# A four-stage token mixer on one core: weight setup that overlaps its transfers, and another order of the work ahead of the state-space scan

## The reference

```
h = attention(x, w_qkv, b_qkv, w_out, b_out)             # 16 heads of 16
h = concat(cls_tok, h)                                   # 513 tokens
h = h + diag_recurrence(layernorm(h))
h = h + ffn(layernorm(h))          # weights: w -> clip(round(w / mean|w|), -1, 1) * mean|w|
h = h + ssm(layernorm(h))
h = h + gated_ffn(layernorm(h))    # w_gate, w_up, w_down quantised in the same way

def ssm(x):
    x_val, z = split(x @ W_in.T)                         # 512 channels each
    x_val = silu(conv4(x_val) + conv_b)
    dt = softplus(x[:, :, :64] @ W_dt.T + b_dt)
    Bm, Cm = x @ W_B.T, x @ W_C.T                        # 16 states
    # for each token: h = exp(dt * A) * h + (dt * x_val) * B ;  y = h . C
    return (scan(x_val, A, Bm, Cm, dt) * silu(z)) @ W_out.T
```

## Time and profile before

| what | value |
|---|---|
| median of 3 runs | 2579.07 us (2574.51 to 2581.37) |
| the profiled execution | 2572.49 us |
| its span | 2570.7 us, 26879 instructions |
| busy share PE / DVE / ACT / POOL | 83% / 80% / 58% / 45% |
| mean granted TensorE clock | 0.951 of full speed |
| span's start to the first scores (L857) | 61.07 us |
| first `taps` to first scan, turn 0 | 357.39 to 390.70 us |

### The profile page before, as it was taken

The page is one execution under the profiler, slowest core; times in us unless marked ns, Lnnn a source line. Parts: engine busy times, 40 slices in busy tenths (PEclk is TensorE's granted clock), DMA queues, the critical chain, the costliest instruction groups (busy, mean ns, idle before and its releaser), DMA issues.

```text
span 2570.7 us, 26879 instructions
## 1 busy us (share of the span) xinstructions
PE 2139.9 (83%) x9364; PEld 1187.4 (46%) x9364; DVE 2067.8 (80%) x2435; ACT 1479.5 (58%) x2358; POOL 1148.7 (45%) x567
## 2 busy tenths in 40 slices
PE   1998888898799887889779898798977988778896
PEld 0326663345333666434542376543453247544354
DVE  6865979996786588999778557999888747799977
ACT  0563558774365446876527544687553754568744
POOL 1220248992222024998222211699722211279952
PEclk9999998999899999999989999899989999989998
DMA  5300000000220000000022000000003100000000
GB/s 183 93 14 1 1 1 1 1 1 1 71 87 1 1 1 1 1 1 1 1 84 75 1 1 1 0 1 1 1 1 113 46 1 1 1 1 0 1 1 17
DMA packets 41088, 51.46 MB, mean 20 GB/s; under 512 B 9072, under 2 KB 32368, under 8 KB 40944
## 3 DMA queue, kind: packets, MB, share of 16 engines
q1 hardware_dynamic: 40944, 49.62, 6.0%
HBM read 26.25 MB, written 10.49 MB: 14 GB/s over the span
## 4 chain that ended last, share of the span: by engine, by line
DVE 43%; PE 37%; issue 8%; ACT 7%; POOL 3%; DMA 1%; SPq 0%; DVEq 0%; ACTq 0%; POOLq 0%
DVE big L1936 16%; PE psum L737 10%; PE psum L884 5%; ACT big L1177 4%; PE psum L872 3%; PE psum L857 3%; PE psum L800 3%; PE psum L1039 3%; DVE mid L1830 3%; ACT mid L1177 2%; DVE big L1608 2%; PE psum L1071 2%; POOL big L2086 2%; DVE mid L1552 2%; DVE negmax L1660 2%
## 5 line engine op out<-in xcount | busy, mean ns | idle before, releaser
L1177 ACT ACTIVATE big<-psum 128x512 f32<-128x512 f32 (+2 forms) x604 | 455.6, 774 | 264.8 <-PE psum L872 141.7
L2086 POOL TENSOR_TENSOR big<-big 128x2048 f32<-128x2048 f32 x124 | 561.8, 4530 | 38.8 <-DVE big L1936 38.6
L1039 PE MATMUL psum<-big,ident 128*128 128x512 f32 x992 | 506.9, 617 | 65.4 <-POOL big L2086 65.4
L1936 DVE TENSOR_TENSOR_SCAN big<-psum,b,big 128x512 f32<-128x512 f32 x404 | 490.3, 1265 | 6.9 <-ACT psum L1177 6.6
L1660 DVE TENSOR_REDUCE negmax<-psum 128x1 f32<-128x512 f32 x512 | 318.7, 678 | 48.3 <-PE psum L857 47.3
L1177 ACT ACTIVATE psum<-mid,aneg 128x512 f32<-128x512 f32 x404 | 268.5, 681 | 79.9 <-DVE big L1936 79.8
L1039 PEld LDWEIGHTS psum<-big,ident 128*128 128x128 f32 x992 | 174.5, 194 | 231.0 <-POOL big L2086 141.8
L857 PE MATMUL psum<-mid 96*128 96x512 bf16 x512 | 189.9, 391 | 33.6 <-DMA mid<-mid 22.8
L872 PE MATMUL psum<-mid 98*128 98x512 bf16 x512 | 181.9, 382 | 20.1 <-ACT big L1177 14.3
L1177 ACT ACTIVATE mid<-mid 128x513 f32<-128x513 f32 (+3 forms) x120 | 104.3, 883 | 154.7 <-DVE mid L1946 80.6
L2051 POOL TENSOR_TENSOR big<-big,mid 128x513 f32<-128x513 f32 x40 | 50.9, 1284 | 288.8 <-ACT big L1177 288.8
(11 more groups left out here) (222 smaller groups left out, 3931.8 us busy)
## 6 DMA issues: line engine op xcount, KB each, us to landing
mid<-mid SPq DMA_DIRECT2D x192, 64.0 KB, 2.5
mid<-scratch SPq DMA_DIRECT2D x192, 64.0 KB, 2.2
scratch<-big SPq DMA_DIRECT2D x4, 1536.0 KB, 5.6
out<-hres SPq DMA_DIRECT2D x8, 513.0 KB, 4.1
big<-in_x SPq DMA_DIRECT2D x8, 512.0 KB, 5.1
big<-in_w SPq DMA_DIRECT2D x2, 1024.0 KB, 6.1
big<-in_wg SPq DMA_DIRECT2D x1, 1024.0 KB, 9.4
big<-in_wu SPq DMA_DIRECT2D x1, 1024.0 KB, 11.3
```

Of the source, the lines that this page charges most:

```text
L1039: mm = nc.tensor.matmul(y_psum[:, c], ident[:, :], st(1, k)[:, c], start=(n == 0), stop=(n == NS - 1))
L1177: return nc.scalar.activation(o, a, func, **kw)
L1936: V.tensor_tensor_scan(st(0, k)[:, c], decays(DT * k + c), bx, b0[:, p, n, c:c + 1], ALU.mult, ALU.add).then_inc(scanned, 1)
L2086: G.tensor_tensor(st(1, k), st(0, k), c_row(k).unsqueeze(1).broadcast_to([P, DT, S]), ALU.mult).then_inc(hc_ready, 1)
```

## The change

**Setup.** Each raw transfer has its own semaphore, and DVE sums each as it lands. The transfer order is: raw, `wq`, `wk`, `vec`, the input of p = 0, then the other weights and the input of p = 1. `turn_start` for the first turn is signalled as soon as SP has issued the first input. The sum over partitions is a matmul with `mean_w` (all 1/256) into bank 7, ahead of the first products on PE. DVE goes twice over each raw tensor (times inverse, min 1; max -1, plus ROUND), and ACT makes the third pass (minus ROUND into bfloat16) after its copies of the first q and k products. PE's turn and DVE's loop wait for `SETUP_ACT`. ACT's copies of the first q and k products stand in `first_copies`, ahead of the turn (in the loop: at the end of the turn before), so ACT's stream has three turns in a loop and the last one written out.

**Lead-up.** `round_up(0)` stands behind both `split_bc`, and `round_up(1)` behind `step_sizes(0)`. The products x(1), z(0), z(1) are interleaved by `IN_ORDER`, with ACT's readers in an order that fits it. The product of dt and x for p = 0 is made on DVE behind `step_sizes(1)`; the one for p = 1 stays on POOL, but waits for DVE's b0.

```diff
@@ -17,7 +17,6 @@
-RADD = bass.bass_isa.ReduceOp.add
@@ -59,7 +58,8 @@
-SETUP_DVE = 8 + 5 + 2 + 15 + 1
+SETUP_DVE = 8 + 5 + 2 + 10 + 1
+SETUP_ACT = 1 + 5
@@ -89,6 +89,11 @@
+IN_ORDER = [("x0", 1), ("x1", 1), ("z0", 0), ("x2", 1), ("z1", 0), ("x3", 1), ("z2", 0), ("z3", 0)]
+IN_ORDER += [(f"z{c}", 1) for c in range(DT)]
@@ -143,8 +148,7 @@
-    order.extend((f"x{c}", 1) for c in range(DT))
-    each(*[f"z{c}" for c in range(DT)])
+    order.extend(IN_ORDER)
@@ -264,7 +268,7 @@
-        wsum = sb("wsum", [P, 8]); wtot = sb("wtot", [P, 8]); wscale = sb("wscale", [P, 8])
+        wsum = sb("wsum", [P, 8]); wscale = sb("wscale", [P, 8])
@@ -436,7 +440,9 @@
-        raw_in = ctx.enter_context(nc.semaphore("raw_in"))
+        raw_in = [ctx.enter_context(nc.semaphore(f"raw_in{n}")) for n in range(5)]
+        qk_weights_in = ctx.enter_context(nc.semaphore("qk_weights_in"))
+        wtot_full = ctx.enter_context(nc.semaphore("wtot_full"))
@@ -544,10 +550,17 @@
+        raws = [big[:, n * raw_n:(n + 1) * raw_n] for n in range(5)]
+        CLAMPED = [8 + 5 + 2 + n for n in (3, 5, 7, 9, 10)]
...
-        plain = [(wq, "wq"), (wk, "wk"), (wv, "wv"), (wo, "wo"), (wa, "wa"), (wB, "wB"), (wC, "wC"), (wx, "wx"),
+        qk_weights = [(wq, "wq"), (wk, "wk")]
+        n_qk = len(qk_weights) + 1
+        plain = [(wv, "wv"), (wo, "wo"), (wa, "wa"), (wB, "wB"), (wC, "wC"), (wx, "wx"),
...
-        n_plain = len(plain) + 3
+        n_plain = len(plain) + 2
+        wtot = psum[:, 7 * BANK:7 * BANK + 8]
@@ -618,22 +631,24 @@
-            def load_x(turn):
-                for p in range(PAIR):
-                    sp.dma_start(xin[:, p], x[turn * PAIR + p].rearrange("k p q -> p k q")).then_inc(x_in[p], 16)
+            def load_x(turn, p):
+                sp.dma_start(xin[:, p], x[turn * PAIR + p].rearrange("k p q -> p k q")).then_inc(x_in[p], 16)
...
-                             v).then_inc(raw_in, 16)
+                             v).then_inc(raw_in[n], 16)
+            for t, name in qk_weights:
+                sp.dma_start(t[:, :, :], w[name].rearrange("(k p) c -> p k c", p=P)).then_inc(qk_weights_in, 16)
+            sp.dma_start(vec[:, :], w["vec"]).then_inc(qk_weights_in, 16)
+            load_x(0, 0)
+            sp.nop().then_inc(turn_start, 1)
...
-            sp.dma_start(vec[:, :], w["vec"]).then_inc(weights_in, 16)
...
-            load_x(0)
-            sp.wait_ge(setup_dve, SETUP_DVE)
-            sp.nop().then_inc(turn_start, 1)
+            load_x(0, 1)
@@ -695,7 +710,8 @@
-                    load_x(i + 1)
+                    for p in range(PAIR):
+                        load_x(i + 1, p)
@@ -716,10 +732,12 @@
-            pe.wait_ge(setup_dve, SETUP_DVE)
-            pe.wait_ge(weights_in, 16 * n_plain)
+            pe.wait_ge(qk_weights_in, 16 * n_qk)
...
+                pe.wait_ge(setup_dve, SETUP_DVE)
+                pe.wait_ge(setup_act, SETUP_ACT)
+                pe.wait_ge(weights_in, 16 * n_plain)
@@ -977,9 +995,9 @@
-                def inputs(name, wt, p):
-                    for c in range(DT):
-                        fill(f"{name}{c}", p, [(wt[:, k, c * P:(c + 1) * P], big_un(p)[:, k]) for k in range(KT)])
+                def inputs(name, p):
+                    wt, c = (wx if name[0] == "x" else wz), int(name[1])
+                    fill(name, p, [(wt[:, k, c * P:(c + 1) * P], big_un(p)[:, k]) for k in range(KT)])
@@ -987,7 +1005,8 @@
-                inputs("x", wx, 0)
+                for c in range(DT):
+                    inputs(f"x{c}", 0)
@@ -1000,9 +1019,8 @@
-                inputs("x", wx, 1)
-                for p in range(PAIR):
-                    inputs("z", wz, p)
+                for name, p in IN_ORDER:
+                    inputs(name, p)
@@ -1164,6 +1182,8 @@
+            pe.wait_ge(setup_dve, 8 + len(raw_w))
+            nc.tensor.matmul(wtot, mean_w[:, :], wsum[:, :], start=True, stop=True).then_inc(wtot_full, 1)
@@ -1180,14 +1200,23 @@
-            act.wait_ge(weights_in, 16 * n_plain)
-            act.wait_ge(setup_dve, 1)
+            act.wait_ge(qk_weights_in, 16 * n_qk)
+            act.wait_ge(setup_dve, 8)
...
-            act.wait_ge(setup_dve, SETUP_DVE)
-            with act.Fori(0, TURNS) as i:
-                act.wait_ge(turn_start, i + 1)
+            def copy_high(p):
+                for name, c in zip(QK_ORDER, QK_PLACE):
+                    wait_full(act, name, p)
+                    run(parts[p][:, 0, c], flat_slot(name, p), ACT.Identity,
+                        bias=col("b" + name[0], int(name[1]))).then_inc(qk_high, 1)
+            def first_copies(turn):
+                act.wait_ge(turn_start, turn + 1)
...
+                load_ln_exp()
+                copy_high(0)
+            def turn_functions():
@@ -1225,12 +1254,7 @@
-                load_ln_exp()
-                for p in range(PAIR):
-                    for name, c in zip(QK_ORDER, QK_PLACE):
-                        wait_full(act, name, p)
-                        run(parts[p][:, 0, c], flat_slot(name, p), ACT.Identity,
-                            bias=col("b" + name[0], int(name[1]))).then_inc(qk_high, 1)
+                copy_high(1)
@@ -1353,8 +1377,8 @@
+                exponential(1)
...
-                exponential(1)
@@ -1363,13 +1387,24 @@
-                for c in range(DT):
-                    first_tap(1, c)
-                    silu(0, c)
-                for c in range(DT):
-                    silu_z(0, c)
-                    silu(1, c)
-                for c in range(DT):
+                first_tap(1, 0)
+                silu(0, 0)
+                first_tap(1, 1)
+                silu(0, 1)
+                silu_z(0, 0)
+                silu(0, 2)
+                first_tap(1, 2)
+                silu(0, 3)
+                silu_z(0, 1)
+                silu(1, 0)
+                first_tap(1, 3)
+                silu_z(0, 2)
+                silu(1, 1)
+                silu_z(0, 3)
+                silu(1, 2)
+                silu_z(1, 0)
+                silu(1, 3)
+                for c in range(1, DT):
@@ -1469,6 +1504,17 @@
+            first_copies(0)
+            for n, ((t, _), raw) in enumerate(zip(raw_w, raws)):
+                act.wait_ge(setup_dve, CLAMPED[n])
+                run(t[:, :, :].rearrange("p k c -> p (k c)"), raw, ACT.Identity, bias=round_bias[:, 1:2]).then_inc(
+                    setup_act, 1)
+            act.wait_ge(setup_act, SETUP_ACT)
+            with act.Fori(0, TURNS - 1) as i:
+                turn_functions()
+                first_copies(i + 1)
+            turn_functions()
@@ -1491,36 +1537,34 @@
-            dve.wait_ge(raw_in, 16 * len(raw_w))
-            raws = [big[:, n * raw_n:(n + 1) * raw_n] for n in range(len(raw_w))]
...
+                dve.wait_ge(raw_in[n], 16)
...
-            dve.wait_ge(setup_pool, SETUP_POOL + 1)
-            affine2(wscale[:, :], wtot[:, :], 1.0 / (HID * D), 1e-5, ALU.mult, ALU.max).then_inc(setup_dve, 1)
+            dve.wait_ge(wtot_full, 1)
+            affine2(wscale[:, :], wtot, 1.0 / HID, 1e-5, ALU.mult, ALU.max).then_inc(setup_dve, 1)
...
-            for n, raw in enumerate(raws):
-                affine2(raw, raw, winv[:, n:n + 1], ROUND, ALU.mult, ALU.add).then_inc(setup_dve, 1)
-            done += len(raws)
-            dve.wait_ge(setup_dve, done)
-            for raw in raws:
-                affine2(raw, raw, ROUND, 1.0, ALU.subtract, ALU.min).then_inc(setup_dve, 1)
-            done += len(raws)
-            dve.wait_ge(setup_dve, done)
-            for (t, _), raw in zip(raw_w, raws):
-                affine2(t[:, :, :].rearrange("p k c -> p (k c)"), raw, -1.0, None, ALU.max).then_inc(setup_dve, 1)
-            done += len(raws)
+            for n in range(len(raws) + 1):
+                if n < len(raws):
+                    affine2(raws[n], raws[n], winv[:, n:n + 1], 1.0, ALU.mult, ALU.min).then_inc(setup_dve, 1)
+                if n:
+                    dve.wait_ge(setup_dve, done + max(2 * n - 2, 1))
+                    affine2(raws[n - 1], raws[n - 1], -1.0, ROUND, ALU.max, ALU.add).then_inc(setup_dve, 1)
+            done += 2 * len(raws)
...
+            dve.wait_ge(qk_weights_in, 16 * n_qk)
...
+            dve.wait_ge(setup_act, SETUP_ACT)
@@ -1837,18 +1881,17 @@
-                round_up(0)
...
-                taps(0, 0)
-                taps(0, 1)
+                round_up(0)
+                for c in range(DT):
+                    taps(0, c)
+                step_sizes(0)
...
-                taps(0, 2)
-                taps(0, 3)
-                step_sizes(0)
@@ -1858,6 +1901,10 @@
+                dve.wait_ge(dt_ready, 1)
+                dve.wait_ge(m_silu, DT)
+                V.tensor_tensor(mid4(0, 3), mid4(0, 2), mid4(0, 0), ALU.mult).then_inc(dtx_ready, 1)
@@ -2007,8 +2054,6 @@
-            pool.wait_ge(setup_dve, 13)
-            G.partition_all_reduce(wtot[:, :], wsum[:, :], P, RADD).then_inc(setup_pool, 1)
@@ -2062,10 +2107,11 @@
```

(8 more changed lines are left out.)

## The result

The changed kernel takes 2545.07 us (median of 4 runs, 2544.26 to 2547.22), against 2580.16 us for the kernel before on the same chip (4 runs, 2574.51 to 2581.37). The ratio is 0.987, with a 95% interval of 0.9852 to 0.9887. The forecast was 2549, in a range of 2535 to 2566. The profiled execution took 2544.26 us; its span is 2542.4.

What follows compares the result with a forecast made beforehand. DVE (43% of the chain) and PE (37%) were taken as the bound, with DVE partly stalled behind POOL. Setup 12.0 plus lead-up 18.0 made 30.0 us, off the 2579.1 median: 2549 us, range 2535 to 2566.

Steps and rivals of the forecast that it cites:

- The setup: Setup, once: ACT's passes behind its q and k copies set the end; first scores at 49.1, 12.0 us earlier.
- The lead-up: Ahead of the scans, four times: DVE's stalls beside POOL's sums fall away; 4.5 us a turn, 18 in all.
- y0 at 383.9, and the scans 2.3 behind it: End of the lead-up: y0 at 383.9 instead of 388.41, scans at 386.2 against 390.70; 4.5 us a turn.
- y0 is held: End of the lead-up: DVE's y0, ready at 382.0, waits for POOL's p = 1 product until 383.9.
- The rival in which it is not held: End of the lead-up: z bounds instead of y0; 6.4 us a turn, 2541.5 us in all; chance 0.14.
- The clock dips in the new gaps: Lead-up, PE's wait before z(0,1): slower tiles leave a gain of 1.2 us a turn, 2562 us; chance 0.13.
- The setup gives 2: Setup: the first input lands late, so only some 2 us are gained there, 2559 us; chance 0.12.
- The stalls only move: Lead-up: stalls pass to another DVE operation beside POOL's sums, the lead-up gives nothing, 2567 us; chance 0.05.
- The slower rival: Lead-up: PE stays at the lower clock through all twelve interleaved tiles, 41 us slower, 2620 us; chance 0.03.

Runs made afterwards that it cites:

- `change`: The changed kernel unaltered, timed again on one chip as the base beside follow-up kernels: 2544.84 us, ratio 0.9885 to the kernel before.
- experiment 2: Against the changed kernel, ScalarE makes the setup's last pass of two raw tensors between its q and k copies, VectorE the fifth: 2538.62 us.
- experiment 1: Against the changed kernel, GpSimd's product for p = 1 waits until VectorE has made y0 too: 2535.83 us, ratio 0.9845 to the kernel before.

## Why the prediction was right

**The setup** was priced at 12.0 us and gave 11.3 at the first scores (12.7 in the two other profiles of the same kernel). Each step can be seen: sums done at 17.04 + 2.29 = 19.3 (18.65 in the sum: the last transfer landed 0.6 later), first product at 20.18 (20.2), ACT free at 30.86 (30.2: first product to fourth copy took 10.7 us, not 10.0; in the profile of `change` 9.3), its passes done at 40.32 (39.6), DVE's split at 40.70 (39.9), scores 9.03 later (9.2). A pass over 2048 columns took 1.99 us, where I took 1.95 from the nearest rows; the 1.99 that the prediction cited from the Trainium skill, "ScalarE: Activation LUTs", section "What ACT_TABLE_LOAD costs", is the measured one. That ACT and not DVE ends the setup was the step that mattered: DVE alone would have promised 14 us; with ACT's passes shared out, experiment 2 has the first scores at 43.85, 17.2 us earlier than before.

**The lead-up** was priced at 4.5 us a turn and gave 5.3. In before's clock (12.0 us more than the new profile's at this place) the steps read: taps from 351.05 (forecast 351.0), `round_up(1)` from 362.7 (362.9), last taps done at 373.5 (373.6), product for p = 0 from 376.1 (376.3), z's silu done at 381.4 (382.0), POOL's product done at 383.4 (383.9). The stalls fell away in full, and ACT's first tap was late next by 0.94 us, as forecast. The term that was mis-sized is "y0 at 383.9, and the scans 2.3 behind it": the 2.3 holds y0's own 0.36 and begins with y0's start, but y0 had started at 381.4 and stood held; it ended 0.16 after POOL, and the scan began 1.98 after POOL's end. With the product's end 0.5 earlier that is the 0.8.

**y0 is held**: right, and shown by experiment 1, where the wait that was changed is the only difference; the rule cited from the Trainium skill, "SBUF — State Buffer", section "Who interferes with whom", agrees with the rows here, down to four columns. The rival in which it is not held fell. **The clock dips in the new gaps**: not there; the idle 1.85 us before z(0,1) brought no lower clock in any of the four turns, and the x and z tiles took 2.00 at most. **The setup gives 2**: the input landed for a first product at 20.18. **The stalls only move**: of the 7.4 us a turn one part did come back, the 1.8 us at y0; the rest is gone, and what lies behind `round_up(0)` was not held. The slower rival needed the clock low through twelve tiles; it was 1.00. (Its sum, 4 x 13 - 12, is 40, not 41.)

**The sum** was 30.0 and is 32.4 in the profile's two stages; the two profiled spans show 28.3 and the medians of three series 35.1, 30.3 and 32.0. The 2549 was 4 us too high. Of the 5.1 us by which the gain of 35.1 exceeds the 30.0, the lead-up gave 3.1 more than priced and the setup 0.7 less; for the other 2.7 no trace has a place. That the forecast lies within 4 us is in part luck, since three series of the same two kernels gave 30.3 to 35.1. The prediction took the 6.6 us between the profiled execution of before and the median as mere spread, while its trace held a stage nobody touched at 35.6 us in two turns and 38.5 in two. Whether that makes the 6.6 is not shown, since only one execution has a trace.

## What to carry to other kernels

Look at an operation's shortest and longest time, not its mean: where one VectorE instruction takes several times its short length (here 6 to 17 times), find what GpSimd was doing then, and start the GpSimd work from a signal behind the short VectorE operations rather than ahead of them. After such a move ask which small two-operand instruction now comes under GpSimd's next long one. And when runs of one kernel differ by more than the change at hand, compare an untouched stage turn by turn: here eight more matmuls that fill TensorE's idle time at one wait were worth a third of the whole edit (11.5 us of 30 to 35).
